# Longer unrolled rounds in the edge scatter of a graph network kernel, with one base update, one reciprocal root and three filler products moved or added

## The reference

```python
h = jnp.maximum(_layernorm(x, axis=-1), 0.0)
x = x + L0(h)   # weighted segment sum over edges + self loops, degree-normalised, 512->128->512
h = jnp.maximum(_layernorm(x, axis=-1), 0.0)
x = x + L1(h)   # mean over a node's edges @ W_l + b + h @ W_r, then h * sigmoid(h)
h = jnp.maximum(_layernorm(x, axis=-1), 0.0)
x = x + L2(h)   # four blocks of attention over the edges and a two-layer relu net
h = jnp.maximum(_layernorm(x, axis=-1), 0.0)
x = x + L3(h)   # two graph attentions, along and against the edges, one product, batch norm, relu
```

## Time and profile before

| | us |
|---|---|
| median of 3 runs | 882.91 (881.9 to 883.12) |
| the profiled execution's own time | 880.6 |
| its span, first to last instruction | 878.6 |
| mean granted TensorE clock | 0.999 of full speed |

### The profile page before, as it was taken

How to read it: one execution, slowest core, us unless ns; L and a number is a source line. 1 busy time by engine, 2 the same in 40 slices (tenths; PEclk the granted TensorE clock), 3 DMA queues, 4 the chain that set the end, 5 groups by cost and what they waited for, 6 DMA issues and landing times.

```text
span 878.6 us, 18172 instructions
## 1 busy us (share of the span) xinstructions
PE 826.9 (94%) x6778; PEld 723.7 (82%) x6778; DVE 623.1 (71%) x1271; ACT 460.1 (52%) x773; POOL 493.6 (56%) x542
## 2 busy tenths in 40 slices
PE   3999989999999999999999999999999999989896
PEld 2999868789898879998887989887898988875565
DVE  7998878964766683576766367577447667689996
ACT  5988675345762434565133466333447634256673
POOL 7354573678433577542466843266674338548871
PEclk9999999999999999999999999999999999999999
DMA  5000102233000142200024310003230002100121
GB/s 162 2 0 0 37 26 85 55 96 115 13 1 13 42 154 85 60 13 1 25 66 130 109 48 1 13 25 117 78 110 13 1 1 85 37 1 32 46 61 59
DMA packets 49760, 44.34 MB, mean 50 GB/s; under 512 B 6013, under 2 KB 37439, under 8 KB 49698
## 3 DMA queue, kind: packets, MB, share of 16 engines
q1 hardware_dynamic: 47234, 39.72, 15.2%
q10 hardware_dynamic: 2464, 3.80, 1.5%
HBM read 42.04 MB, written 1.33 MB: 49 GB/s over the span
## 4 chain that ended last, share of the span: by engine, by line
PE 70%; DVE 17%; ACT 6%; issue 3%; DMA 2%; DVEq 1%; POOL 0%; SPq 0%; ACTq 0%
PE psum L1822 20%; PE psum L1816 18%; PE psum L1927 13%; PE psum L1897 6%; PE psum L1846 5%; DVE arena L2349 3%; ACT arena L1618 2%; DVE arena L1013 2%; PE psum L2112 2%; PE psum L2109 2%; PE psum L1870 2%; PE psum L877 1%; PE psum L935 1%; DVE stats L2472 1%; DVE hot_dst L1050 1%
## 5 line engine op out<-in xcount | busy, mean ns | idle before, releaser
L1360 POOL TENSOR_SCALAR acc<-acc,rden,flag 128x628 f32<-128x628 f32 x80 | 69.5, 868 | 119.4 <-DVE rden L2345 119.4
L1927 PE MATMUL psum<-ringw,arena 128*128 128x512 f32 (+1 forms) x480 | 119.3, 397 | 4.0 <-DVE arena L2357 2.5
L1822 PE MATMUL psum<-arena 128*128 128x384 f32 (+5 forms) x675 | 115.8, 324 | 0.0
L1816 PE MATMUL psum<-arena,ringw 128*128 128x314 f32 x768 | 114.3, 310 | 0.1
L1816 PEld LDWEIGHTS psum<-arena,ringw 128*128 128x128 f32 x768 | 112.9, 190 | 1.5 <-DVE arena L2322 1.1
L1822 PEld LDWEIGHTS psum<-arena 128*128 128x128 f32 (+1 forms) x675 | 104.8, 189 | 7.1 <-DVE arena L2349 1.1
L1927 PEld LDWEIGHTS psum<-ringw,arena 128*128 128x128 f32 (+1 forms) x480 | 86.8, 186 | 25.6 <-DVE arena L2357 3.5
L1816 PE MATMUL psum<-arena 128*128 128x314 f32 (+1 forms) x480 | 87.7, 321 | 7.3 <-DVE arena L2349 6.9
L1816 PEld LDWEIGHTS psum<-arena 128*128 128x128 f32 (+1 forms) x480 | 70.5, 187 | 15.8 <-DVE arena L2349 14.1
L2322 DVE SCALAR_TENSOR_TENSOR arena<-psum,cols,arena 128x628 fp32r<-128x628 f32 x32 | 27.9, 872 | 75.8 <-ACT arena L1600 75.8
L1431 POOL TENSOR_TENSOR ringw<-raw,ringw 128x512 fp32r<-128x512 f32 x56 | 71.6, 1288 | 15.5 <-ACT ringw L1659 15.5
(11 more groups left out here) (313 smaller groups left out, 1840.6 us busy)
## 6 DMA issues: line engine op xcount, KB each, us to landing
raw<-in_L_gnn_m_w SPq DMA_DIRECT2D x16, 256.0 KB
xn<-in_L_gnn_m_w SPq DMA_DIRECT2D x16, 256.0 KB
raw<-in_L_gnn_wv SPq DMA_DIRECT2D x8, 256.0 KB
xn<-in_L_gnn_wv SPq DMA_DIRECT2D x8, 256.0 KB
raw<-in_L_gnn_wq SPq DMA_DIRECT2D x8, 256.0 KB
xn<-in_L_gnn_wq SPq DMA_DIRECT2D x8, 256.0 KB
raw<-in_L_gnn_wk SPq DMA_DIRECT2D x8, 256.0 KB
xn<-in_L_gnn_wk SPq DMA_DIRECT2D x8, 256.0 KB
```

The source lines that it names most:

```text
L1360: g.tensor_scalar(pbuf[:, k % 4, 0:NW], pbuf[:, k % 4, 0:NW], rden[:, k:k + 1], flag[:, 1, k % NT:k % NT + 1], ALU.mult, ALU.mult).then_in ...
L1816: ins = pe.matmul(big[buf(u)][0:l.shape[1], h, 0:HW], l, r[:, h * HW:(h + 1) * HW], start=(i == 0), stop=(i == len(terms) - 1))
L1822: ins = pe.matmul(to, l, r, start=(i == 0), stop=(i == len(terms) - 1))
L1927: ins = pe.matmul(brow(ROWBLK[f"{name}{t}"])[0:KEYS[t], :], l, r, start=(pieces[0] + i == 0), stop=(pieces[-1] == KT - 1 and i == len(term ...
```

## The change

Four edits. PE's scatter loop has a body of 20 groups in place of four, so it runs two rounds of a pass and not ten; the loops of DVE, ACT and POOL keep their four. DVE's step of `base_f` for a next pass moves from behind the last `hot` to the pass's opening, behind the copy to `base_i`. In POOL's list the second tile's root comes ahead of `left_rest(3)` and the third tile's ahead of `bias_added(4)`. In L3 PE runs three products of ones between the spread `first_branch(0)` and the spread `maxima(EARLY)`, after a wait for the reading of the fourth forward tile.

```diff
+ROUND = 20
+assert NG % ROUND == 0 and ROUND % HOT == 0
...
             second_branch(1)
             first_branch(0)
+            pe.wait_ge(h_read, 2 * NT - 1)
+            idle_products(pe, 2 * NBIG, 3)
             maxima(EARLY)
             first_branch(1)
             pe.wait_ge(one_up, 2)
...
             left_rest(2)
-            rstd_of(LN_L1, NT)
+            for t in range(2):
+                rstd_of(LN_L1 + t, NT + t)
             left_rest(3)
-            rstd_of(LN_L1 + 1, NT + 1)
+            rstd_of(LN_L1 + 2, NT + 2)
             bias_added(4)
-            for t in range(2, NT):
+            for t in range(3, NT):
                 rstd_of(LN_L1 + t, NT + t)
...
             with pe.Fori(0, passes + 1) as kp:
-                with pe.Fori(0, NG // HOT) as gi:
-                    for b in range(HOT):
-                        c = kp * NG + gi * HOT + b + 1
+                with pe.Fori(0, NG // ROUND) as gi:
+                    for q in range(ROUND):
+                        b = q % HOT
+                        c = kp * NG + gi * ROUND + q + 1
...
                 dve.tensor_copy(base_i[:, :], base_f[0:1, :]).then_inc(pass_up, 1)
+                dve.tensor_scalar(base_f[0:1, :], base_f[0:1, :], float(WIN), float(NP), ALU.add, ALU.min).then_inc(pass_up, 1)
                 for b in range(HOT - 1):
                     hot(b, b)
...
                 dve.tensor_scalar(dst_rel[:, :, :], dst_rel[:, :, :], float(WIN), None, ALU.subtract).then_inc(pass_up, 1)
-                dve.tensor_scalar(base_f[0:1, :], base_f[0:1, :], float(WIN), float(NP), ALU.add, ALU.min).then_inc(pass_up, 1)
                 for b in range(HOT):
                     add(NG - HOT + b, b)
```

## The result

| | before | after |
|---|---|---|
| median, us | 882.27 (881.64 to 883.12, 6 runs) | 889.87 (888.96 to 891.87, 6 runs) |
| ratio | | 1.0089, interval 1.0075 to 1.0103 |
| profiled execution, span, us | 880.6, 878.6 | 891.87, 889.9 |

The change made the kernel 7.6 us slower, far outside the predicted range and at the place that the prediction's rival 2 named.

The account below looks back on a forecast made before the run. It took DVE and POOL to bound the scatter, DVE's chain the second stretch and DVE L3. Terms -0.24 - 0.55 + 0.45 = -0.34 us on the median 882.91 gave 882.6, range 881.1 to 884.3.

Parts of the forecast that it names:

- rival 2: Scatter, group 20: branching back over 2,400 instructions means a long fetch, +8.1 us, about 890.7; chance 0.06 beyond 5 us.
- PE's rounds of twenty: Scatter loop: eight of ten seams go, 3.9 us of PE's time that PE can't use; one seam stays at group 20.
- I take 2 us: Seam at group 20: the assumed stall for fetching the new body, between one packet's 1.1 us and 11 us for ten.
- The free 2.9 us: Seam at group 20: PE ready about 65.7, may start at 68.65, so up to 2.9 us of stall cost nothing.
- The scatter's other term, -0.24 us: End of the scatter: the last add starts at 102.62 instead of 102.86; ends -0.5 and +0.4 us.
- rival 1: Scatter: PE's seams were the bound, so all 3.9 us come and the time is 878.9; chance 0.06.
- The base's step: DVE's step moved to the pass's opening: costs 0.13 us there, ends 0 and 0.86, and frees little at the end.
- The roots: Second stretch: second root ahead of POOL's remainder shortens the first normalising to 0.53 us; -0.55, between -0.2 and -0.65.
- Rival 4: Second stretch: the roots give nothing, as the remainder meets the second normalising instead; 883.1 or so, chance 0.08.
- The products of ones: L3, between the spreads: three products take 0.8 us and delay DVE's maximum at 786; +0.45 us, ends 0 and +0.6.
- They can give nothing back by the clock: L3: the products of ones save nothing, because PE's granted clock is already at its upper level there.
- rival 3: L3: the products between the spreads cost nothing if DVE catches up; 882.1, chance 0.12.

Follow-up runs that it names:

- e1: The kernel before with only PE's scatter loop put in rounds of twenty groups; 890.53 us, ratio 1.0098 (1.0083 to 1.0112).
- e6: The kernel before with PE's scatter loop in rounds of sixteen groups, the last eight groups written out behind; 890.60 us, ratio 1.0087.
- e4: The kernel before with all forty groups in one body, so PE never branches back within the pass; 882.75 us, ratio 1.0007.
- e5: The kernel before with PE's scatter loop in rounds of twelve groups, the last four groups written out behind; 884.78 us, ratio 1.0027.
- e7: The kernel before with the order of the roots in POOL's list alone changed; 881.31 us, ratio 0.9994 (0.9984 to 1.0003).
- e8: The kernel before with the three products of ones between the spreads alone; 881.97 us, ratio 0.9998 (0.9989 to 1.0007).
- e2: The changed kernel with PE's rounds of four groups again, keeping base's step, roots and products of ones; 881.39 us, ratio 0.9991.
- e9b: The kernel before with the base's step at the pass's opening alone; 881.34 us, ratio 0.9997 (0.9988 to 1.0006).

## Why the prediction was wrong

**The step that failed is the seam at group 20, in "PE's rounds of twenty".** The prediction saw that the body grows to 2,400 instructions, knew the rule by which they are fetched again, and then wrote "I take 2 us", with "up to 2.9 us of stall at that seam are free". The stall was far longer, and part of the free time was spent before it came.

- *The stall.* It is 4.18 + 2.56 us of silence, and with the half clock behind it 8.3 us of PE's time; by the same measure 7.6 in e1 and 7.8 in e6. The 2 us stood between one packet's 1.1 us and ten packets in turn, and no row supported it. The chance of a long stall, 0.06, rested on "most of them unseen", which is true of packets in a straight line only (e4).
- *The free 2.9 us.* At the seam that room was about right, but the prediction let the stall have all of it. PE came to group 19 late already, 64.93 - 27.61 = 37.32 us behind the base's copy, against 63.08 - 27.59 = 35.49 in e5, and 36.44 in e1. The silences of the first round did that in these two; e4, with the same code up to there, has 35.49 as well. What was left were 0.9 us in after (DVE's adds are 7.4 us late for 8.3 of PE's) and 1.8 in e1 (5.8 for 7.6). And PE, which was to run the later groups in 1.67 us each, was still late at the end: the last adds waited for it, 1.9 us more in after, 0.7 in e1 and 1.7 in e6. The terms close: in after 1.8 + 8.3 - 2.7 of room + 1.9 = 9.3 us, in e1 1.0 + 7.6 - 2.8 + 0.7 = 6.5.

Rival 2 named the mechanism, the place and the time (890.7 against 889.87), but that the time came out is luck: its working was wrong. It took the ten packets one after the other. The runs show two fetches in turn, the rest beside the work, a clock at half and a late end: the errors cancel. e6 shows it, with less code to fetch and the same stall.

**The scatter's other term, -0.24 us, was 0.** All rounds whose code is held, and e4, give 74.37 to 74.43 us, e7 74.50. That PE's seams don't set the pace was right, and rival 1 fell. PE's own end came as predicted too: in e4 its last group starts 71.82 us behind the copy, 0.46 earlier than in before. But I had the last add come earlier with it, held only by a repeat of the 0.89 us of DVE's sequencer, and it stands 1.26 us behind the add before it in before and 1.27 in e4. There PE's signal came at 101.44, 0.7 us ahead of that add. The instruction records of DVE's sequencer show the place: between two of its register steps for this add it stands 0.4 us, in before and e4 alike, and 0.04 between the same steps of the three adds ahead. Why it stands there stays open.

The reading behind this term was too narrow as well. The 7.31 us between the adds of groups 28 and 32 hold from the seventeenth add on; over the first sixteen DVE takes 6.98 us a round, in before and after, which is less than PE's 7.17. PE had the slack for that, so nothing came of it.

**The base's step**, +0.13, was +0.06 us at the opening; away from POOL's product the step took 0.17 us, which fits the neighbour as the reason for the 0.86 but doesn't show it by itself, and nothing came of freeing the end.

**The roots**, -0.55, were right: 0.52 us for the first normalising in place of 1.12, and a gain of 0.6 us that lasts in all five profiles. The median of e7 is 0.7 lower, though its interval takes in no change. Rival 4 fell, in the trace: the second normalising takes 0.51 us in after.

**The products of ones**, +0.45, were right as a wait (0.43 and 0.44 us, 0.5 in DVE's list) and wrong as a price: e8 is 0.05 us under before. "They can give nothing back by the clock" rested on one profile of before, which happened to be one of two without the fall. So rival 3's number came true for another reason than it gave: DVE caught up nothing.

Without the rounds the prediction's terms give -0.55 + 0.45 + 0.13 = +0.03; e2 measured -1.1, with an interval from -1.6 to -0.1. One end of the range was added up wrong: -0.5 - 0.65 + 0 on 882.91 is 881.8, not 881.6. Nothing hangs on it.

## What to carry to other kernels

Before unrolling a hardware loop, count the instructions of its body, loads and waits included, and the blocks that it lies in: here a body of 1,440 in seven blocks stayed held, and one of 1,920 in nine was fetched anew at its one branch back, for some 8 us. Unroll to well under that or all the way, and don't expect a gain where the engine isn't the bound: the medians of the rounds of eight and forty lie 0.2 to 0.6 us above that of before, and those of twelve 2 to 3 us above it for a reason that stays open. And where a kernel's rule is known and its price isn't, the missing price belongs in the range at its far end: an invented middle value is not a bound.

## What the runs showed that was not expected

- A branch back over a body that is no longer held stopped TensorE twice, 3.9 to 4.2 us and then, after a single product, 2.3 to 2.6 us, whether the body has 1,920 or 2,400 products and loads. The granted clock was at its 1.2 GHz level from about the moment when it resumed, for 6.4 us in e6, 6.8 in e1 and 7.8 in after.
- The packets that come again number the blocks in which the body lies (nine and eleven), one more than its length alone would give.
- Straight code could be run at nearly PE's own pace (e1, 1.68 us a group) or with a silence of up to 0.7 us at the edge of a block, every 125 products, that the profile calls "issue".
- In L3 the granted clock fell to about half in eight of ten profiles in a stretch in which that of before shows 1.00. One profile's clock is not that of the runs.
- Two profiles can differ by a neighbour. At 145 us DVE's masks (L2688) take 0.82 us alone, and twice as long when a remainder of POOL starts just ahead of one. In before POOL's came 0.07 us behind it:

```profile
145.74 0.82 DVE L2688 SCALAR_TENSOR_TENSOR mask<-mask,acc 128x640 f32<-128x640 f32 x1
145.81 1.91 POOL L1444 TENSOR_TENSOR condw<-xn,condw 64x512 fp32r<-64x512 f32 x1 [1.25 <-ACT condw L1659]
```

In e9b it came ahead, the same mask took 1.82 us, and that profile, 0.95 us ahead of before at the last add, is level with it from 146.5 us on. The profile of before is the exception: in all thirteen others DVE loses 1.0 to 1.1 us against it between 145.2 and 146.5 us of its time. That is a part of the 11.3 us between the two profiles.

```profile
144.61 1.29 POOL L1444 TENSOR_TENSOR condw<-xn,condw 64x512 fp32r<-64x512 f32 x1 [1.02 <-ACT condw L1659]
144.76 1.82 DVE L2688 SCALAR_TENSOR_TENSOR mask<-mask,acc 128x640 f32<-128x640 f32 x1
```
